# Cell stage of a perceiver kernel: edge weights stored transposed and paired with the second weights, one transfer a pair

## The reference

```python
for c in range(6):                                # nodes
    nsrc = min(c + 1, 5)
    snode = c - nsrc
    eq, ek, ev = (lind + nsrc - 1, lind, lind + nsrc // 2)      # three of the 20 edges
    in_q, in_k, in_v = (c - 1, snode, snode + nsrc // 2)
    q = ew[c, 0] * (nodes[in_q] @ We[eq] + be[eq])
    k = ew[c, 1] * (nodes[in_k] @ We[ek] + be[ek])
    v = ew[c, 2] * (nodes[in_v] @ We[ev] + be[ev])
    o = _mha(q, k, v, Wq[c], Wk[c], Wv[c], Wo[c])               # q @ Wq etc., 8 heads, softmax, @ Wo
    nodes[c] = act_w[c] * o + q
    lind += nsrc
return _layernorm(nodes[5], ln_g, ln_b)
```

## Time and profile before

| | us |
|---|---|
| device time, median of 3 runs | 3146.64 |
| device time, lowest and highest | 3142.65, 3150.09 |
| span of the profiled execution, first to last instruction | 3135.8 |
| PE busy | 2953.1 (94%) |
| DVE busy | 2154.7 (69%) |
| ACT busy | 2032.0 (65%) |
| cell stage: first transfer issued | 1601.88 |
| cell stage: first matmul of the preparation, first of the loop's input | 1607.18, 1670.98 |
| cell stage: last edge matmul (L2153) | 2665.5 |

### The profile page before, as it was taken

One profiled execution on the slowest core, in us unless ns is written; L12 is line 12 of the kernel. 1 busy time (PEld: TensorE's weight loads), 2 busy tenths in 40 slices (PEclk: granted clock), 3 DMA queues, 4 the chain that ended last, 5 costly groups with the idle time before them and its releaser, 6 DMA issues. The chain is left out here.

```text
span 3135.8 us, 85575 instructions
## 1 busy us (share of the span) xinstructions
PE 2953.1 (94%) x32401; PEld 2419.5 (77%) x32401; DVE 2154.7 (69%) x5336; ACT 2032.0 (65%) x4177; POOL 1173.9 (37%) x1035
## 2 busy tenths in 40 slices
PE   8999999889999999999979999999999998798899
PEld 7777777677787777887867887887787887565798
DVE  5777777666666666666635788778788777568543
ACT  6788888677776766777724766666666666333444
POOL 6888888576665655655610000000000000111210
PEclk9999999999999999999989999999999999899899
DMA  2111112067888887987973111111111110552000
GB/s 87 47 50 55 47 59 68 13 118 134 152 150 144 149 138 143 155 145 139 181 201 119 36 43 54 34 43 56 50 43 49 49 36 21 180 165 78 8 21 27
DMA packets 643033, 273.32 MB, mean 87 GB/s; under 512 B 549387, under 2 KB 617952, under 8 KB 642736
## 3 DMA queue, kind: packets, MB, share of 16 engines
q1 hardware_dynamic: 613168, 225.13, 34.3%
q10 hardware_dynamic: 29568, 44.05, 4.2%
HBM read 113.37 MB, written 21.50 MB: 43 GB/s over the span
## 5 line engine op out<-in xcount | busy, mean ns | idle before, releaser
L1330 POOL TENSOR_TENSOR front_parts<-wide_prob,front_parts 128x1024 f16<-128x1024 f32 x256 | 549.1, 2146 | 380.1 <-ACT front_parts L1556 326.3
L1649 DVE TENSOR_REDUCE wide_row_max<-wide_score 128x1 f32<-128x1024 f32 x256 | 312.8, 1222 | 170.8 <-PE wide_score L1368 170.0
L1368 PE MATMUL wide_score<-wide_kT,wide_qT 128*128 128x512 f32 x1536 | 417.9, 408 | 4.4 <-ACT wide_prob L1544 2.8
L1544 ACT ACTIVATE wide_prob<-wide_score,wide_neg_max 128x1024 f32<-128x1024 f32 x256 | 285.2, 1114 | 159.7 <-DVE wide_neg_max L1652 153.8
L1368 PEld LDWEIGHTS wide_score<-wide_kT,wide_qT 128*128 128x128 f32 x1536 | 279.8, 191 | 65.6 <-issue 8.9
L894 ACT ACTIVATE mask_prob<-mask_prob,mask_row_min 128x256 f32<-128x256 f32 x512 | 255.4, 503 | 86.4 <-DVE mask_row_min L976 85.7
L618 POOL TENSOR_TENSOR mask_prob<-mask_prob,mask_inv_sum 128x512 f32<-128x512 f32 x256 | 265.4, 1042 | 56.4 <-DVE mask_inv_sum L1027 54.9
L1556 ACT ACTIVATE front_parts<-wide_prob 128x1024 f16<-128x1024 f32 x256 | 269.7, 1054 | 13.6 <-ACT wide_prob L1544 7.1
L117 POOL TENSOR_TENSOR cell_var_eps<-cell_mean_var,const_eps 128x4 f32<-128x4 f32 x8 | 1.6, 202 | 655.3 <-DVE cell_mean_var L111 655.3
L2492 DVE TENSOR_REDUCE cell_row_max<-cell_score 128x8 f32<-128x512 f32 x192 | 131.2, 683 | 148.1 <-PE cell_score L2117 146.1
L1384 PE MATMUL wide_turn<-front_probT,wide_v 128*128 128x256 f16 x1536 | 191.2, 275 | 2.6 <-DMA front_probT<-front_parts 2.6
(11 more groups left out here) (367 smaller groups left out, 7039.7 us busy)
## 6 DMA issues: line engine op xcount, KB each, us to landing
cell_w_stage<-cell_weights ACTq DMA_DIRECT2D x24, 768.0 KB, 5.8
mask_ctx<-in_ctx SPq DMA_DIRECT2D x32, 512.0 KB, 3.8
ctx_ctx<-in_ctx SPq DMA_DIRECT2D x32, 512.0 KB, 4.1
mask_mask<-in_mask_BxS_ik SPq DMA_DIRECT2D x32, 256.0 KB, 3.8
front_probT<-front_parts SPq DMA_TRANSPOSE x512, 3.2
cell_w_stage<-in_L_ffn_We ACTq DMA_DIRECT2D x24, 256.0 KB, 2.8
cell_w_stage<-in_L_ffn_Wo ACTq DMA_DIRECT2D x24, 256.0 KB, 3.2
front_x_all<-in_x SPq DMA_DIRECT2D x32, 128.0 KB, 2.1
```

Source lines behind the costliest of these rows:

```text
L1330: pool.tensor_tensor(parts[:, s % 2, LO, :], prob[:, s % 2, :], parts[:, s % 2, HI, :], ALU.subtract).then_inc(part_lo, 1)
L1368: mm = pe.matmul(score[:, s % 2, half * 512:(half + 1) * 512], qT[:, u_par, a, s * P:(s + 1) * P], kT[:, par, b, half * 512:(half + 1) * 5 ...
L1544: act.activation(prob[:, s % 2, :], score[:, s % 2, :], ACT.Exp, bias=neg_max[:, s % 2:s % 2 + 1], scale=SHARP, accum_out=row_sum[:, u_par ...
L1649: dve.tensor_reduce(row_max[:, one], score[:, s % 2, :], AX.X, ALU.max).then_inc(max_found, 1)
```

## The change

The tables of edges and sources move into a function of their own, `cell_edges`, with the same numbers (not shown). The host hands over the weights in another layout (`laid_out`). `W_pairs` holds for each pair the edge matrix, already transposed, and the second matrix beside it: 128 partitions with one run of 4 KB. `W_own` holds for each node the plain edge matrix and `Wo` in the same way, and `b_columns` the edge biases as columns. SP loads a pair by one transfer of 512 KB. The same memory as before is now eight places of one pair each, and a place is filled again when its pair's product is done. PE's transposes (T), ACT's copies, `be_rows` and `weT` are gone. The products go round four `score` banks instead of two. ACT issues one transfer of 512 KB for a node's own matrices instead of two of 256 KB, and issues the first one as its first instruction in the stage.

```diff
-def stage_cell(nc, mem, const, x_in, ew, act_w, W_e, b_e, W_q, W_k, W_v, W_o, ln_g, ln_b, x_out):
-    NODES, PREV, HEADS = W_q.shape[0], 5, 8
+def stage_cell(nc, mem, const, x_in, ew, act_w, W_pairs, W_own, b_columns, ln_g, ln_b, x_out):
...
-    weT = z[:, :, :].rearrange("p (x h) o -> p x h o", x=2)
...
-    raw_loaded = [[mem.sem(f"raw_loaded{i}{f}") for f in range(3)] for i in range(2)]
-    be_ready = mem.sem("be_ready")
-    be_copied = mem.sem("be_copied")
-    we_turned = mem.sem("we_turned")
-    we_copied = mem.sem("we_copied")
+    raw_loaded = [mem.sem(f"raw_loaded{i}") for i in range(8)]
...
+    PAIRS = 3 * NODES
+    RAW_EDGE, RAW_W = 0, MAT
...
-    raw_places = [prob[:, :, :, :].rearrange("p x r t -> p (x r t)"), probT[:, :, :].rearrange("p r t -> p (r t)"),
-                  v[:, :, :, :, :].rearrange("p x s b d -> p (x s b d)")]
-    def raw_w(c, m):
-        buf, at = (raw_places[0], m) if c % 2 == 0 else (raw_places[1 + m // 4], m % 4)
-        return buf[:, at * MAT:(at + 1) * MAT].rearrange("p (h o) -> p h o", h=DH)
+    raw_places = ([prob[:, x // 2, x % 2 * 2:x % 2 * 2 + 2, :].rearrange("p r t -> p (r t)") for x in range(4)]
+                  + [probT[:, x * 2:x * 2 + 2, :].rearrange("p r t -> p (r t)") for x in range(2)]
+                  + [v[:, x].rearrange("p s b d -> p (s b d)") for x in range(2)])
+    RAW = len(raw_places)
+    def raw(n, at):
+        return raw_places[n % RAW][:, at:at + MAT].rearrange("p (h o) -> p h o", h=DH)
...
-        def load_raw(c, f):
-            for m, w in ((RAW_EDGE + f, W_e[edge[c][f]]), (RAW_W + f, (W_q, W_k, W_v)[f][c])):
-                sp.dma_start(raw_w(c, m), w.rearrange("(h p) o -> p h o", p=P)).then_inc(raw_loaded[c % 2][f], 16)
-        sp.dma_start(be_rows[:, :], b_e).then_inc(w_loaded, 16)
-        load_raw(0, 0)
+        def load_pair(n):
+            sp.dma_start(raw_places[n % RAW], W_pairs[n]).then_inc(raw_loaded[n % RAW], 16)
+        def store_set(c):
+            sp.wait_ge(staged, c + 1)
+            sp.dma_start(set_dram[(c - 1) % NODES], made_of(c)).then_inc(stage_stored[c % 2], 16)
+        load_pair(0)
+        sp.dma_start(be[:, :, :], b_columns).then_inc(w_loaded, 16)
         sp.dma_start(ew_sb[:, :], ew.rearrange("c t -> (c t)").partition_broadcast(P)).then_inc(w_loaded, 16)
         sp.dma_start(act_sb[:, :], act_w.partition_broadcast(P)).then_inc(w_loaded, 16)
-        load_raw(0, 1)
-        load_raw(0, 2)
+        for n in range(1, 5):
+            load_pair(n)
         sp.dma_start(x_ln[:, :, :], block_rows(x_in[0:BLK, :])).then_inc(x_loaded, 16)
-        for f in range(3):
-            load_raw(1, f)
+        for n in range(5, RAW):
+            load_pair(n)
         sp.dma_start(g_row[:, :], ln_g.partition_broadcast(P)).then_inc(rows_loaded, 16)
         sp.dma_start(b_row[:, :], ln_b.partition_broadcast(P)).then_inc(rows_loaded, 16)
-        for c in range(2, NODES + 2):
-            if c < NODES:
-                sp.wait_ge(fused_ready, 3 * (c - 1))
-                for f in range(3):
-                    load_raw(c, f)
-            sp.wait_ge(staged, c - 1)
-            sp.dma_start(set_dram[(c - 3) % NODES], made_of(c - 2)).then_inc(stage_stored[c % 2], 16)
+        for n in range(RAW, PAIRS):
+            sp.wait_ge(fused_ready, n - RAW + 1)
+            load_pair(n)
+            if (n - RAW) % 3 == 2:
+                store_set((n - RAW) // 3)
+        for c in range((PAIRS - RAW) // 3, NODES):
+            store_set(c)
...
-        for h in range(DH):
-            mm = pe.transpose(prep_banks[2][:, h * EDGES:(h + 1) * EDGES], be_rows[:, h * P:(h + 1) * P], ident[0:EDGES, 0:EDGES])
-        mm.then_inc(be_ready, 1)
-        pe.wait_ge(be_copied, 1)
-        for c in range(NODES):
-            for f in range(3):
-                n = 3 * c + f
-                raw_here(pe, c, f)
-                if n >= 2:
-                    pe.wait_ge(we_copied, n - 1)
+        for n in range(PAIRS):
+            e = edge[n // 3][n % 3]
+            pe.wait_ge(raw_loaded[n % RAW], 16 * (n // RAW + 1))
+            for oh in range(DH):
+                at = n * DH + oh
                 for mh in range(DH):
-                    for ih in range(DH):
-                        mm = pe.transpose(prep_banks[n % 2][:, mh * D + ih * P:mh * D + (ih + 1) * P],
-                                          raw_w(c, RAW_EDGE + f)[:, ih, mh * P:(mh + 1) * P], ident[:, :])
-                mm.then_inc(we_turned, 1)
-                for oh in range(DH):
-                    at = n * DH + oh
-                    for mh in range(DH):
-                        mm = pe.matmul(prep_banks[3][:, at:at + 1], raw_w(c, RAW_W + f)[:, mh, oh * P:(oh + 1) * P],
-                                       be[:, mh, edge[c][f]:edge[c][f] + 1], start=(mh == 0), stop=(mh == DH - 1))
-                pe.wait_ge(we_copied, n + 1)
-                if n >= 2:
-                    pe.wait_ge(fused_done, n - 1)
-                for ih in range(DH):
-                    for mh in range(DH):
-                        mm = pe.matmul(score[n % 2][:, ih * D:(ih + 1) * D], weT[:, n % 2, mh, ih * P:(ih + 1) * P],
-                                       raw_w(c, RAW_W + f)[:, mh, :], start=(mh == 0), stop=(mh == DH - 1))
-                mm.then_inc(fused_ready, 1)
+                    mm = pe.matmul(bias_bank[:, at:at + 1], raw(n, RAW_W)[:, mh, oh * P:(oh + 1) * P], be[:, mh, e:e + 1],
+                                   start=(mh == 0), stop=(mh == DH - 1))
+            if n >= ROW:
+                pe.wait_ge(fused_done, n - ROW + 1)
+            for ih in range(DH):
+                for mh in range(DH):
+                    mm = pe.matmul(score[n % ROW][:, ih * D:(ih + 1) * D], raw(n, RAW_EDGE)[:, mh, ih * P:(ih + 1) * P],
+                                   raw(n, RAW_W)[:, mh, :], start=(mh == 0), stop=(mh == DH - 1))
+            mm.then_inc(fused_ready, 1)
...
-            for at, w in ((EDGE_AT, W_e[edge[c][0]]), (OUT_AT, W_o[c])):
-                act.dma_start(w_stage[:, at:at + MAT].rearrange("p (h o) -> p h o", h=DH), w.rearrange("(h p) o -> p h o", p=P)).then_inc(set_loaded, 16)
-        act.wait_ge(be_ready, 1)
-        act.activation(be[:, :, :].rearrange("p h e -> p (h e)"), prep_banks[2][:, 0:DH * EDGES], ACT.Copy).then_inc(be_copied, 1)
-        for n in range(3 * NODES):
-            if n == 4:
-                load_own(0)
-                act.wait_ge(staged, 1)
-                act.activation(w_set[:, HI, FUSED_AT:SET], w_stage[:, FUSED_AT:SET], ACT.Copy).then_inc(set_hi, 2)
-            act.wait_ge(we_turned, n + 1)
-            if n >= 2:
-                act.wait_ge(fused_ready, n - 1)
-            act.activation(weT[:, n % 2].rearrange("p h i -> p (h i)"), prep_banks[n % 2][:, :], ACT.Copy).then_inc(we_copied, 1)
+            act.dma_start(w_stage[:, 0:FUSED_AT], W_own[c]).then_inc(set_loaded, 16)
+        load_own(0)
+        act.wait_ge(staged, 1)
+        act.activation(w_set[:, HI, FUSED_AT:SET], w_stage[:, FUSED_AT:SET], ACT.Copy).then_inc(set_hi, 2)
...
-            act.wait_ge(set_loaded, 32 if isinstance(number, int) and number == 1 else number * 48)
+            act.wait_ge(set_loaded, 16 if isinstance(number, int) and number == 1 else number * 32)
...
-        dve.wait_ge(be_copied, 1)
...
-                ins = dve.tensor_scalar(made[:, f * MAT:(f + 1) * MAT], score[n % 2][:, :], ew_sb[:, n:n + 1], None, ALU.mult)
+                ins = dve.tensor_scalar(made[:, f * MAT:(f + 1) * MAT], score[n % ROW][:, :], ew_sb[:, n:n + 1], None, ALU.mult)
...
+def laid_out(np, inputs):
+    a = {name: np.asarray(value) for name, value in inputs.items()}
+    def halves(w):
+        return w.reshape(DH, P, -1).transpose(1, 0, 2)
+    edge = cell_edges()[0]
+    W_e, W_o = a.pop("L0_ffn_We"), a.pop("L0_ffn_Wo")
+    W_qkv = [a.pop("L0_ffn_" + w) for w in ("Wq", "Wk", "Wv")]
+    pairs_of = [np.stack([halves(W_e[edge[c][f]].T), halves(W_qkv[f][c])], axis=1) for c in range(NODES) for f in range(3)]
+    a["L0_ffn_W_pairs"] = np.stack(pairs_of).reshape(3 * NODES, P, -1)
+    own = [np.stack([halves(W_e[edge[c][0]]), halves(W_o[c])], axis=1) for c in range(NODES)]
+    a["L0_ffn_W_own"] = np.stack(own).reshape(NODES, P, -1)
+    a["L0_ffn_b_columns"] = a.pop("L0_ffn_be").reshape(-1, DH, P).transpose(2, 1, 0)
+    return a
```

34 lines of the change are left out of this document (17 added, 17 removed).

## The result

| kernel | median us | runs | lowest to highest |
|---|---|---|---|
| before, all runs of the study | 3139.4 | 113 | 3129.97 to 3151.69 |
| changed, three measurements | 3122.9 | 19 | 3117.43 to 3128.47 |

The three ratios to the kernel before are 0.9946 [0.9929, 0.9963], 0.9937 [0.9923, 0.9951] and 0.9954 [0.9935, 0.9973]: faster by about 0.54%, some 16.5 us. The forecast was 3138.2 (3131.5 to 3144.0), a gain of 8.4.

The account below looks back on a forecast made before the run. PE was taken to bound the cell's preparation. Gains of 9.1 - 1.2 + 0.5 = 8.4 us took the span from 3135.8 to 3127.4; plus 10.84 this made 3138.2 us, range 3131.5 to 3144.0.

Parts of the forecast that it names:

- The runs' median lies 10.84 above the span and I keep that.: Last step: 10.84 us added to the forecast span of 3127.4 to give the time, 3138.2 us.
- Steady pairs: PE, pairs 2 to 17: without transposes a pair costs 0.85 + 1.83 = 2.68 us (2.58 to 2.78); the copy's removal gives nothing.
- Stall on the banks: PE's single 0.71 us wait for DVE in the preparation goes with four banks, with 3.5 us to spare.
- The cold pairs: First pairs at half clock: bias step's 0.69 us goes, pair 0 takes 4.95, pair 1 ends 8.3 us after PE's start.
- The start: PE's first matmul of the preparation comes 1.2 us later, as ACT's early 512 KB share the engines; bounds -0.5 and +1.9.
- Loads, stores, the rest behind the pairs: Later pairs' loads and the stores cost nothing; PE's 3.31 us of idleness after the pairs stays.
- The loop: One ACT transfer less in each of 24 slots saves some 0.02 us a slot, 0.5 us; bounds 0 and 2.
- From there to the end of the span all the same but 0.5 us.: After the preparation's last product, nothing changes up to the span's end except 0.5 us.
- (a): Rival: DMA paces the preparation, 237 GB/s; gain 5.8 + 0.5, time 3140.3, up to 3142; chance 0.13.
- (c): Rival: PE stays at 1.2 GHz through the preparation, waiting for each pair's transfer; 3156.4 with eight such pairs; chance 0.04.
- (d): Rival: pairs cost PE what they did, by a slower product or a returning wait; 3145.9; chance 0.07.
- (b): Rival: clock rises 3 us sooner at the start or doesn't fall at 1672; 3135.0 to 3136.7; chance 0.12.

Follow-up runs that it names:

- two_banks: The changed kernel with a pair's product in one of two banks instead of four; 3127.98 us, 0.9956 of the kernel before.
- late_own: The changed kernel with node 0's own 512 KB issued after node 0 is staged, not as ACT's first transfer; 3119.9 us, 0.9936 of the kernel before.
- all_three: The changed kernel with node 0's own matrices late, one bias product, 26 identity transposes before pair 0 and 10 behind pair 17; 3118.6 us.
- warm_start: The changed kernel with 26 identity transposes on PE before pair 0, while PE waits for its transfers; 3118.61 us, 0.9937 of the kernel before.

## Why the prediction was wrong

**The step that failed first is its last:** "The runs' median lies 10.84 above the span and I keep that." The 10.84 compared a profiled execution of some 3137.5 us with a median of three high runs; what lies around the span is 1.7 us before and 1.9 in the changed kernel. The 8.4 us taken off the usual 3139.4 would have given 3131.0. That is 7.2 of the 15.3 us by which 3138.2 missed 3122.9; the other 8.1 are gain that the sum did not have. The first error alone does not account for the miss: with the range moved down by 7.2, to 3124.3 to 3136.8, the measured time is still below it. Of the 8.1 the preparation's terms missed 2.3 and the stretch behind the loop, put at nothing, 1.6; the rest is not located.

**Steady pairs.** T at 0.43 us was right (0.44). "The copy is hidden by B ... it costs PE nothing" was wrong by 0.06 us a pair. S and B together were 2.62, inside my 2.58 to 2.78: 16 x 0.06 = 1.0 us.

**Stall on the banks.** It went, as forecast. It was worth a little more than the 0.71 us of the row: in S-to-S starts of the old profiles the pair takes 3.93 instead of 3.12, and with faster pairs the stall would have been 4.81 - 2.62 = 2.19 (two_banks).

**The cold pairs.** PE's start to its last S's start took 47.7 us; the forecast was 51.2 - 1.83 = 49.4. Of the 1.7 us the shorter periods are 1.0; the rest is the clock, which rose 4.7 us behind PE's start, not 6.4, so pair 1 began at full clock.

**The start.** Later by 1.2 us was right in the mean (the terms given, 1.7 less 0.4, make 1.3): from SP's first issue to PE 6.4 to 7.2 us in three changed profiles (mean 6.9), 5.3 to 6.2 in five old ones (mean 5.7). The single pair of profiles showed my upper bound, 1.9. The reason given holds for pair 0 alone: it lands 5.0 to 5.4 us behind its issue in the eleven profiles in which node 0's 512 KB are issued beside it and both have rows of 4 KB, and they land within 0.2 us of it; without them it is 4.1 and 3.7 us (late_own, all_three). The trace agrees here with the Trainium skill, "DMA: Bandwidth & Descriptors", section "Issuing engines are not separate DMA queues": transfers started from different engines interleave on the same 16 DMA engines. But PE waited for act_w, which landed later than pair 0, and that took 5.0 us in late_own and 7.7 in all_three, with the same late matrices. So what sets the start is open, and the right 1.2 is in part luck.

**Preparation in all.** -0.3 and -9.9 us against a forecast of 7.9: the mechanism right, the size 2.3 too small, 1.3 with early rises of the clock alone. In the first pair of profiles PE's start to its last S's start fell from 58.51 to 47.73, by 10.78 us where the sum had 9.1: 17 pairs at 0.50, the stall at 0.78 with what the next pair gave back, the bias step 0.69 and pair 0 0.86 (5.86 to 5.00). The start takes 1.9 us of that back in this pair, 1.1 in the means.

**Loads, stores, the rest behind the pairs.** No wait on a pair and none on a store; the rest stayed at 3.30 us. As forecast.

**The loop.** 0.5 us can't be told: 993.7 to 997.0 us in the changed kernel, 993.9 to 1002.3 in the old ones. The copy of v came 0.05 us sooner in the slot read, 1.2 us over 24, within my bounds.

**"From there to the end of the span all the same but 0.5 us."** Wrong: 1.6 us behind the loop, in every kernel with packed pairs and none without. They lie in block 0 of the context stage, which lands later where an instruction packet falls on SP's first issues; why it falls there is open. 0.6 more up to the scan is within the scatter.

**Rivals.** (a), DMA as the pace, is refuted: share 0.32 late in the preparation. (c), slower by the clock, too; PE did stay at half clock for 10.3 to 12.3 us of steady work in some profiles, one of them of the old preparation, but without a pause between pairs. (d) is refuted by the periods. (b) has a part: the mean granted clock was 0.9770 over 107 runs of the kernel before and 0.9781 over the 19 of the changed one. At (1 - clock) x 2 x span that is 144 us at half clock against 137. If PE worked in all of it, half would be the price, an estimate of 3.7 us at most, of the 16.2. In the profiles PE was busy at half clock for 85 to 102 us in the five old ones (mean 93.5) and 83 to 95 in the three changed (mean 87.8), which makes 2.8 of the 13.9 us; 0.8 of that lies in the pairs of the preparation, the rest is no larger than the scatter of each stage.

So of 16.2 us: 10.2 in the preparation (9.2 with the clock's rise alike) and 1.6 behind the loop are located in stages; some 4.4 us lie in differences no larger than the scatter of one profile, which the clock may hold in part. That is where the cause stays open.

## What to carry to other kernels

Before taking off a gain, compare the profiled execution's own time with the runs: here it stands 1.7 to 2.0 us above its span, and a difference beyond that is scatter of runs and no part of the kernel. The copy that ended 0.05 us ahead of its reader was not free here (0.06 us a pair); give "just hidden" a bound of its own. When PE is the bound, removing its instructions gives their duration, and a price read from one stall is only right for the speed at which it was read. One profile of each kernel is not enough for a difference of 1 or 2 us: look how the granted clock stood in both first.

## What was unexpected of the hardware

- The granted clock after a rest of PE of 10 to 14 us rose either 4.7 to 6.6 us (ten profiles) or 8.2 to 12.3 us (seven) behind PE's first matmul of the stage, with the same kind of work behind it; no edit here decides which.
- It also fell while PE was at work: in warm_start at 1610.3 for 6.8 us, 8 us behind PE's first transpose and 1.7 us into pair 0. What it answers no run shows.
- 128 rows of 4 KB a pair moved at 389 to 407 GB/s in the windows shown, 512 rows of 1 KB at 348, with the DMA share at 1.02 and 1.10.
- One of SP's issues took 1.15 to 1.94 us instead of 0.43 in the six profiles where a 16 KB instruction packet began 0.2 to 0.3 us ahead of it, and ended within 0.4 us of the packet's end.
